# First graph: weights, splits and mask spread over four places and GpSimd; last graph: late low parts on VectorE, output projection in two parts

## The chip, the cores and the metric

The kernel runs on one core of one Trainium2 chip. A core has TensorE (PE) for matrix products, VectorE (DVE), ScalarE (ACT) and GpSimd (POOL) for elementwise work, and SyncE (SP), which here issues every DMA. The engines run their own instruction streams in order and wait for each other by semaphores. The metric is the device time of one execution in microseconds (us); lower is better.

## The reference

Two layers over 32 graphs of 512 nodes with 512 features, in float32. Cut to what matters:

```python
def layer0(x, adj, W, a):                 # W: 512 x 256
    h = x @ W                             # 512 x 256
    e = leaky_relu(h @ a[0] + (h @ a[1]).T, 0.2) + (-1e9) * (1 - adj)
    out = softmax(e) @ h
    return concatenate([out, h], -1)      # 512 x 512
def layer1(x, adj):                       # 8 heads of 64
    q, k, v = (heads(x @ Wn.T + bn) for n in "qkv")
    s = where(adj == 0, -inf, q @ k.T / 8)
    return (softmax(s) @ v).merge_heads() @ Wo.T + bo
x = layernorm(x + layer0(x, adj, W, a))
x = layernorm(x + layer1(x, adj))
```

## The kernel before, in words

Every operand of a product is split into a high part (rounded to fp32r) and a low part (the rest), and a product is three products: high by high, high by low, low by high (`PARTS`). ScalarE makes the high part (`split_hi`), VectorE or GpSimd the low part by a subtraction. Tokens lie in four tiles of 128 nodes, features in four chunks.

The work on a graph is cut into pieces with short names. The order in which each engine does them is written out by hand in tables: `TENSOR_PLAN`, `SCALAR_PLAN`, `VECTOR_PLAN`, `GPSIMD_PLAN` and `SP_PLAN` for a middle round, `LAST_..._PLAN` for the last graph, `..._PROLOGUE` and `..._START` for the first graph, `..._ENDING` for what follows the last graph. Rounds overlap: a round does attention of one graph (layer 1), the first layer of the next and the first loads of the one after.

Pieces that matter here, first layer: `A` splits the transposed input tile, `B` is `x @ W` (h, and the two attention terms from 2 extra columns of the weight), `N` spreads one term over all partitions, `pre` adds and leaks, `red` applies the mask and takes the row maximum, `aexp` is exp, `C` transposes and splits, `D` multiplies by h, `lst`/`lrs` are layer statistics, `lap` applies the layer norm, `E` transposes the result. `w0` to `w3` split Wq, Wk, Wv and Wo. Second layer: `q`, `k`, `V`, `W` are projections (`V` and `W` are the two halves of v), `scores` the products of two heads with one query tile, `reduce` mask and row maximum, `exp` the exponential, `vt` VectorE's 32 by 32 block transpose. Probabilities are finished in eight groups a graph (ph 0 to 7, four tiles each). `sv` stores a group to DRAM and `mv` loads it back turned; `hi` and `lo` split it (two instructions of 1024 columns each a group); `weigh` multiplies by v (two a group, 16 matmuls each group's pair); `lows`, `sum`, `norm` and `turn` add the halves, divide and split the result into `oT`. `O0` to `O3` are the output projection, `evO` adds it to the tokens, `yst`/`yrs` are the second layer's statistics, `fin` applies them and the tile is stored.

Waits that matter: `weigh` of group ph needs both `lo` of the group and, at its first half, the `sum` of the group before; the fourth `vt` of group ph needs the `weigh` of group ph-2 done, and `hi` needs the `weigh` of the group before done, since `turned_hi_prob` is one buffer. `load_sums` (`rl`) of group ph waits for `norm` of ph-1.

At the start, W and `a` are loaded, VectorE forms the extra weight columns with eight reductions, ScalarE splits W, VectorE makes its low part, then the mask of four tiles from `adj`. The four weights come one after another through two places: `tokens[2]` (after the mask was built from it) and `blocked[:, 0]`; each load waits for the low part of an earlier one. ScalarE has `w0 w1` at the end of `SCALAR_START`, ahead of piece `N`, and VectorE has them ahead of `red0`. A bias product `bb` (bv times Wo) stands ahead of `E0` on PE.

## Time and profile before

| | us |
|---|---|
| median of 3 runs | 3027.59 (3025.34 to 3031.99) |
| profiled execution, its own time | 3028.9 |
| span of the profiled execution | 3027.1 |
| PE busy | 2937.6 (97%) |
| DVE busy | 2611.6 (86%) |
| ACT busy | 2417.9 (80%) |
| POOL busy | 1996.2 (66%) |
| mean granted TensorE clock | 0.989 |

The busy time of PE is modelled from pipelined matmuls, so 97% says that PE hardly ever waits, not that it is at its peak. In the 40 slices of the page PE shows 9 tenths in all but the first and the last (5 and 5). The rest of the text is on these two slices, of 75.7 us each, and on what lies between them.

### The profile page before, as it was taken

What the parts mean: (1) busy time and instruction counts of PE and PEld (TensorE: products, weight loads), DVE (VectorE), ACT (ScalarE), POOL (GpSimd) and SP (SyncE); (2) the same over time, 40 slices, a digit from 0 to 9 for tenths busy, and PEclk for the clock granted to TensorE, in tenths of its full rate; (3) what the DMA queues carried; (4) which work ended last, traced back from release to release, by engine and by line L of the source; (5) the groups of instructions that cost most, each with busy time, mean ns of one, the idle gap of its engine ahead of it and who ended that gap; (6) DMA issues with size and microseconds to landing.
All of it is one profiled execution on the core that took longest, in us unless ns stands there. A gap on an engine that the chain in (4) does not pass through costs nothing.

```text
span 3027.1 us, 58284 instructions
## 1 busy us (share of the span) xinstructions
PE 2937.6 (97%) x19084; PEld 2507.9 (83%) x19084; DVE 2611.6 (86%) x6556; ACT 2417.9 (80%) x5031; POOL 1996.2 (66%) x1415
## 2 busy tenths in 40 slices
...
GB/s 132 206 224 232 239 242 231 225 225 233 237 250 228 224 226 229 243 243 230 221 222 235 239 243 227 229 225 240 238 238 223 228 235 232 242 236 227 218 210 149
DMA packets 306413, 685.39 MB, mean 226 GB/s; under 512 B 56896, under 2 KB 90432, under 8 KB 273344
## 3 DMA queue, kind: packets, MB, share of 16 engines
...
## 4 chain that ended last, share of the span: by engine, by line
PE 82%; DMA 5%; ACT 4%; DVE 4%; POOL 3%; issue 2%; SPq 1%; ACTq 0%; DVEq 0%; POOLq 0%
PE R_bank L646 47%; PE O_bank L735 14%; PE S_bank L716 11%; PE L_bank L646 6%; PE L_bank L637 3%; DMA turned_lo_prob<-scratch 3%; POOL turned_lo_prob L1093 2%; DVE blocked L1033 1%; DMA r_wide<-r_scratch 1%; DVE prob L1013 1%; ACT turned_hi_prob L764 1%; DMA scratch<-blocked 1%; ACT prob L852 1%; ACT tokens L781 1%; SPq L567 1%
## 5 line engine op out<-in xcount | busy, mean ns | idle before, releaser
L1093 POOL TENSOR_TENSOR turned_lo_prob<-turned_lo_prob,turned_hi_prob 128x1024 fp32r<-128x1024 f32 x512 | 1230.0, 2425 | 493.0 <-ACT turned_hi_prob L764 492.5
L852 ACT ACTIVATE prob<-prob,small_cols 128x512 f32<-128x512 f32 x1024 | 728.4, 715 | 89.4 <-DVE small_cols L1013 86.1
L1033 DVE STREAM_TRANSPOSE blocked<-prob 128x512 f32<-128x512 f32 x1024 | 697.6, 699 | 54.1 <-PE O_bank L735 34.7
L1013 DVE CUSTOM_DVE_ANT_0 prob<-S_bank,mask 128x512 f32<-128x512 f32 x1024 | 669.4, 681 | 31.6 <-PE S_bank L716 27.7
L735 PE MATMUL O_bank<-turned_hi_prob,v_st 128*128 128x256 f32 x2048 | 521.2, 291 | 32.7 <-POOL turned_lo_prob L1093 32.4
L764 ACT ACTIVATE turned_hi_prob<-turned_lo_prob 128x1024 fp32r<-128x1024 f32 x512 | 522.0, 1051 | 31.1 <-DMA turned_lo_prob<-scratch 27.7
L735 PE MATMUL O_bank<-turned_lo_prob,v_st 128*128 128x256 f32 x2048 | 507.8, 285 | 0.0
L735 PEld LDWEIGHTS O_bank<-turned_hi_prob,v_st 128*128 128x128 f32 x2048 | 394.1, 192 | 58.9 <-POOL turned_lo_prob L1093 52.3
L716 PE MATMUL S_bank<-qk_pair 64*128 64x512 f32 x3072 | 435.5, 411 | 6.8 <-DVE small_cols L1013 5.4
L646 PE MATMUL R_bank<-wv,x1T 128*128 128x256 f32 x3072 | 398.7, 285 | 0.0
L735 PEld LDWEIGHTS O_bank<-turned_lo_prob,v_st 128*128 128x128 f32 x2048 | 394.9, 193 | 3.9
L646 PEld LDWEIGHTS R_bank<-wv,x1T 128*128 128x128 f32 x3072 | 377.6, 189 | 12.5 <-issue 12.4
L646 PE MATMUL R_bank<-wo,oT 128*128 128x512 f32 x1536 | 382.3, 401 | 1.3 <-POOL oT L1107 1.3
L646 PE MATMUL R_bank<-x1T,wq 128*128 128x512 f32 x1536 | 379.9, 396 | 1.0 <-DVE v_st L909 1.0
L646 PE MATMUL R_bank<-x1T,wk 128*128 128x512 f32 x1536 | 380.2, 396 | 0.7 <-DVE v_st L909 0.7
L1107 POOL TENSOR_TENSOR oT<-o_half,oT 128x256 fp32r<-128x256 f32 x256 | 189.5, 740 | 244.5 <-ACT oT L764 244.1
L716 PEld LDWEIGHTS S_bank<-qk_pair 64*128 64x128 f32 x3072 | 266.8, 185 | 100.5 <-issue 27.5
L646 PEld LDWEIGHTS R_bank<-x1T,wk 128*128 128x128 f32 x1536 | 288.9, 188 | 72.3 <-DVE v_st L909 1.1
L646 PEld LDWEIGHTS R_bank<-wo,oT 128*128 128x128 f32 x1536 | 280.5, 188 | 75.5 <-issue 11.1
L646 PEld LDWEIGHTS R_bank<-x1T,wq 128*128 128x128 f32 x1536 | 282.3, 188 | 62.1 <-issue 1.4
L777 ACT ACTIVATE qk_pair<-R_bank,b_cols 128x512 fp32r<-128x512 f32 x256 | 172.4, 684 | 171.0 <-PE R_bank L646 169.6
L1087 POOL TENSOR_TENSOR o_half<-o_half,r_wide 128x256 f32<-128x256 f32 x256 | 189.1, 739 | 103.1 <-DVE o_half L1041 95.4
...
## 6 DMA issues: line engine op xcount, KB each, us to landing
scratch<-blocked SPq DMA_DIRECT2D x256, 1024.0 KB, 4.3
turned_lo_prob<-scratch SPq DMA_DIRECT2D x256, 1024.0 KB, 5.8
tokens<-xT SPq DMA_DIRECT2D x128, 256.0 KB, 5.2
tokens<-x SPq DMA_DIRECT2D x128, 256.0 KB, 2.9
r_wide<-r_scratch SPq DMA_DIRECT2D x512, 64.0 KB, 3.2
out<-tokens SPq DMA_DIRECT2D x128, 256.0 KB, 4.2
r_scratch<-r_cols SPq DMA_DIRECT2D x256, 16.0 KB
...
```

Of the source, the lines that this page charges most:

```text
L637: last = pe.transpose(bank[:, c * P:(c + 1) * P], src[:, c * P:(c + 1) * P], ident[:, :])
L646: last = pe.matmul(dst, stationary(s, c), moving(m, c), start=(c, s, m) == todo[0], stop=(c, s, m) == todo[-1])
L716: last = pe.matmul(score_bank(R, 2 * u + w)[:, :], qk_pair[own, qp, t * P:(t + 1) * P], qk_pair[own, 2 + kp, :], start=j == 0, stop=j == 2)
L735: last = pe.matmul(O_bank[:, o_cols(w)], v_st[:, c, (2 * (ph // 2) + w) % HEADS, :], probs, start=(c, s) == todo[0], stop=(c, s) == todo[-1])
L764: act.activation(dst, src, ACT.Copy).then_inc(done, 1)
L777: act.activation(hi_ap, bank_ap, ACT.Identity, bias=b_col[:, pair % 4:pair % 4 + 1]).then_inc(qk_hi, 1)
L852: act.activation(prob_tile(R, s), prob_tile(R, s), ACT.Exp, bias=negmax[:, slot:slot + 1], scale=-1.0, accum_out=psum_row[:, ph % 2, j:j + ...
L1013: dve.tensor_tensor_reduce(prob_tile(R, s), score_bank(R, s)[:, :], mask[:, s % 8 // 2, :], -SCALE, HUGE, ALU.add, ALU.min, negmax[:, slot ...
L1033: dve.transpose(blocked[:, ph % 2, :, :, 2 * (s % 2) + s % 4 // 2, :].rearrange("p d c i -> p c d i"), prob_tile(R, s).rearrange("p (d c i ...
L1087: pool.tensor_tensor(o_half[:, :], o_half[:, :], r_wide[:, :], ALU.mult).then_inc(o_normed, 1)
L1093: pool.tensor_tensor(lo_ap, lo_ap.bitcast(F32), turned_hi_prob[:, 2 * a:2 * a + 2, :, :].bitcast(F32), ALU.subtract).then_inc(p_lo, 1)
L1107: pool.tensor_tensor(oT[:, LO, u // 2 % 4, o_cols(u % 2)], o_half[:, :], oT[:, HI, u // 2 % 4, o_cols(u % 2)].bitcast(F32), ALU.subtract). ...
```

## The change

First graph. The four weights get four staging places, `blocked[:, 0]`, `blocked[:, 1]`, `tokens[1]` and `tokens[2]`, and a semaphore each. `adj`, Wv and Wq are issued right behind the first inputs, the small biases last. GpSimd builds the mask and the low parts of W (its first 256 columns), Wq and Wo; VectorE makes the low parts of the four input tiles, of Wk and of Wv. ScalarE touches its activation table at the very start, and splits the first 256 columns of W before the extra columns are known. `w0` to `w3` move behind the first layer's `pre` and `aexp`. The addition to the tokens (`X`) no longer stands between the pieces `B`. The bias product `bb` moves behind the first scores, into `O_bank`.

Last graph. For groups 4 to 7 the low part of the probabilities is made by VectorE (`vlo`) and not by GpSimd. O0 to O3 stand together ahead of `weigh0`. Ahead of the last two `weigh`, PE does three of the four chunks of the final output projection (`P0` to `P2`, then `P3`) into the score banks, which are free by then, and `O0` to `O3` are the fourth chunk alone. The last statistics are in two halves (`yrs`, `yrs1`), so that `fin0` and `fin1` need only tiles 0 and 1.

The middle rounds' tables are as they were.

```diff
@@ tables (a few of the lines)
-    "w0 w1",
+    "X0 X1 X2 X3",
-GPSIMD_START = (
-    "A0 A1 A2 A3",
-)
+GPSIMD_START = ()
 SCALAR_PROLOGUE = (
-    "N pre0 pre1 pre2 aexp0 aexp1 C0 w2",
+    "N pre0 pre1 pre2 aexp0 aexp1 C0 pre3",
+    "C1 aexp2 aexp3 C2 w2 C3 w0 w1",
...
 GPSIMD_PROLOGUE = (
-    "lrs A0 A1 bo0 A2 bo1 bo2 A3",
-    "bo3",
+    "lrs w0 w3 A0 A1 A2 A3 bo0",
+    "bo1 bo2 bo3",
 TENSOR_ENDING = (
-    "weigh weigh O0 O1 O2 O3",
+    "P0 P1 P2 weigh weigh P3 O0 O1",
+    "O2 O3",
 VECTOR_ENDING = (
-    "sum evO0 evO1 yst0 evO2 yst1 yst2 evO3",
-    "yst3 yrs0",
+    "sum evO0 evO1 yst0 yst1 evO2 evO3 yrs",
+    "yst2 yst3 yrs1",
+DVE_WEIGHTS = (1, 2)
+LAST_LO = 8
@@ staging
+        def weight_stage(j):
+            if j % 2 == 1:
+                return (blocked[:, 0, :, :, :, :].rearrange("p d c j i -> p (d c j i)").rearrange("p (c n) -> p c n", c=C),
+                        tokens[2][:, :, :])[j // 2]
+            return (tokens[1][:, :, :],
+                    blocked[:, 1, :, :, :, :].rearrange("p d c j i -> p (d c j i)").rearrange("p (c n) -> p c n", c=C))[j // 2]
@@ sync
-            for j, w in enumerate((WqT, WkT, WvT, WoT)):
-                if j == 0:
-                    sp.wait_ge(mask_built, 1 + T)
-                else:
-                    sp.wait_ge(w_lo, j)
-                place = tokens[2][:, :, :] if j % 2 == 0 else stage().rearrange("p (c n) -> p c n", c=C)
...
+            load_weight(2, WvT)
+            load_weight(0, WqT)
+            for i in range(T):
+                load_tokens(start, i)
+            sp.wait_ge(w_lo[0], 2)
+            load_weight(1, WkT)
+            sp.wait_ge(mask_built, 1 + T)
+            load_weight(3, WoT)
@@ tensor
                 if kind == "N":
                     pe.wait_ge(terms_ready, R.nx(4, 4))
-                    pe.wait_ge(solo_done, R.nx(len(SOLO), 4))
+                    if not R.prologue:
+                        pe.wait_ge(solo_done, R.nx(len(SOLO), 4))
...
+                if kind == "P":
+                    if i == 0:
+                        pe.wait_ge(s_red, R.n(32, 0))
+                        pe.wait_ge(o_lo, R.n(8, -2))
+                    for c in range(C - 1):
+                        for s, m in PARTS:
+                            pe.matmul(S_bank[i][:, :], oT[:, s, c, i * P:(i + 1) * P], wo[:, m, c, :],
+                                      start=(c, s, m) == (0,) + PARTS[0], stop=False)
+                if kind == "O" and R is end:
+                    pe.wait_ge(o_lo, R.n(8, i // 2 - 1))
+                    for s, m in PARTS:
+                        last = pe.matmul(S_bank[i][:, :], oT[:, s, C - 1, i * P:(i + 1) * P], wo[:, m, C - 1, :],
+                                         start=False, stop=(s, m) == PARTS[-1])
+                    last.then_inc(ring_mm, 1)
@@ scalar
+            act.wait_ge(mask_built, 1)
+            act.activation(a_sum[:, :], minus_half[:, :], ACT.Copy).then_inc(act_ready, 1)
             act.wait_ge(w_loaded[0], 16)
+            split_hi(w0[:, HI, :, 0:F1], w_stage()[:, :, 0:F1], w_hi[0])
             act.wait_ge(wa_done, 2 * C)
-            split_hi(w0[:, HI, :, :], w_stage(), w_hi)
-            act.wait_ge(small_loaded, SMALL)
+            split_hi(w0[:, HI, :, F1:F1 + 2], w_stage()[:, :, F1:F1 + 2], w_hi[0])
@@ vector
+                if kind == "A" and R is start:
+                    dve.wait_ge(turned_hi, R.n2(4, i + 1))
+                    split_lo(turned_part(R, "A", i, LO), tokens[R.buffer(2)][:, i, :].rearrange("p (c t) -> p c t", c=C),
+                             turned_part(R, "A", i, HI), turned_lo)
...
+            def probs_lo(R, m):
+                if m == LAST_LO:
+                    dve.wait_ge(p_lo, R.n(16, m))
+                ph, a = m // 2, m % 2
+                dve.wait_ge(p_hi, R.n(16, m + 1))
+                split_lo(turned_lo_prob[:, ph % 2, 2 * a:2 * a + 2, :, :],
+                         turned_lo_prob[:, ph % 2, 2 * a:2 * a + 2, :, :].bitcast(F32),
+                         turned_hi_prob[:, 2 * a:2 * a + 2, :, :], p_lo)
@@ gpsimd
+                if kind == "w" and i not in DVE_WEIGHTS:
+                    w = (wq, wk, wv, wo)[i]
+                    pool.wait_ge(w_hi[1 + i], 1)
+                    pool.tensor_tensor(w[:, LO, :, :], weight_stage(i), w[:, HI, :, :].bitcast(F32),
+                                       ALU.subtract).then_inc(w_lo[1 + i], 1)
...
-            pool.wait_ge(small_loaded, SMALL)
+            pool.wait_ge(w_hi[0], 1)
+            pool.tensor_tensor(w0[:, LO, :, 0:F1], w_stage()[:, :, 0:F1], w0[:, HI, :, 0:F1].bitcast(F32),
+                               ALU.subtract).then_inc(w_lo[0], 1)
+            pool.wait_ge(adj_loaded, 16)
             pool.wait_ge(mask_built, 1)
+            for t in range(T):
+                pool.tensor_scalar(turned_keys(mask[:, t, :]), by_key_place(tokens[2][:, t, :].bitcast(I32)), 0.0, MASKED,
+                                   ALU.is_equal, ALU.mult).then_inc(mask_built, 1)
```

ScalarE in the first graph, from the high parts of h on. Before (`wq`, `wk`, `wv` are the weights' high parts, `n_wide` is piece N, `prob` the first layer's attention, `x1T` pieces C):

```order
L764 ACTIVATE h<-S_bank 128x256 [waits solo_mm] x4
L764 ACTIVATE wq<-tokens 128x2048 [waits w_loaded1]
L764 ACTIVATE wk<-blocked 128x2048 [waits w_loaded2]
L813 ACTIVATE n_wide<-L_bank 128x512 [waits n_mm]
L809 ACTIVATE prob<-n_wide,terms 128x512 [waits n_copied]
L809 ACTIVATE prob<-n_wide,terms 128x512 x2
L816 ACTIVATE prob,a_cols<-prob,a_cols 128x512 [waits a_red] x2
L764 ACTIVATE x1T<-L_bank 128x4x128 [waits solo_mm]
L764 ACTIVATE wv<-tokens 128x2048 [waits w_loaded3]
```

Now:

```order
L796 ACTIVATE h<-S_bank 128x256 [waits solo_mm] x4
L847 ACTIVATE n_wide<-L_bank 128x512 [waits n_mm]
L843 ACTIVATE prob<-n_wide,terms 128x512 [waits n_copied]
L843 ACTIVATE prob<-n_wide,terms 128x512 x2
L850 ACTIVATE prob,a_cols<-prob,a_cols 128x512 [waits a_red] x2
L796 ACTIVATE x1T<-L_bank 128x4x128 [waits solo_mm]
L843 ACTIVATE prob<-n_wide,terms 128x512 [waits solo_mm]
L796 ACTIVATE x1T<-L_bank 128x4x128 [waits solo_mm]
L850 ACTIVATE prob,a_cols<-prob,a_cols 128x512 [waits a_red] x2
L796 ACTIVATE x1T<-L_bank 128x4x128 [waits solo_mm]
L796 ACTIVATE wv<-blocked 128x2048 [waits w_loaded3]
L796 ACTIVATE x1T<-L_bank 128x4x128 [waits solo_mm]
```

The high parts of Wq and Wk stood between h and `n_wide`; now no weight stands ahead of the second `x1T`, and Wv, Wq, Wk and Wo come in one stretch after the attention of the first layer.

TensorE at the end of the program. Before (`turned_lo_prob` with `v_st` is the last `weigh`, `wo` with `oT` the output projection):

```order
L735 MATMUL O_bank<-turned_lo_prob,v_st 128x256
L646 MATMUL R_bank<-wo,oT 128x512 [waits o_lo,ring_done]
L646 MATMUL R_bank<-wo,oT 128x512 x8
L646 MATMUL R_bank<-wo,oT 128x512 [waits o_lo]
L646 MATMUL R_bank<-wo,oT 128x512 x2
L646 MATMUL R_bank<-wo,oT 128x512 [waits ring_done]
L646 MATMUL R_bank<-wo,oT 128x512 x11
L646 MATMUL R_bank<-wo,oT 128x512 [waits ring_done]
L646 MATMUL R_bank<-wo,oT 128x512 x11
L646 MATMUL R_bank<-wo,oT 128x512 [waits ring_done]
L646 MATMUL R_bank<-wo,oT 128x512 x11
```

Now, from the last matmul of `weigh13` to the first of `weigh14`, and from `P3` on:

```order
L767 MATMUL O_bank<-turned_lo_prob,v_st 128x256
L722 MATMUL S_bank<-wo,oT 128x512 [waits o_lo,s_red]
L722 MATMUL S_bank<-wo,oT 128x512 x26
L767 MATMUL O_bank<-turned_hi_prob,v_st 128x256 [waits o_sum,p_lo]
...
L767 MATMUL O_bank<-turned_lo_prob,v_st 128x256
L722 MATMUL S_bank<-wo,oT 128x512 x9
L727 MATMUL S_bank<-wo,oT 128x512 [waits o_lo]
L727 MATMUL S_bank<-wo,oT 128x512 x2
L727 MATMUL S_bank<-wo,oT 128x512 [waits o_lo]
L727 MATMUL S_bank<-wo,oT 128x512 x2
L727 MATMUL S_bank<-wo,oT 128x512 [waits o_lo]
L727 MATMUL S_bank<-wo,oT 128x512 x2
```

Of 48 matmuls of the last output projection 36 moved ahead of the last `oT` half: 27 stand between `weigh13` and `weigh14`, 9 behind `weigh15`; 12 are left behind the wait for `o_lo`.

VectorE at the same place. Before (`r_cols` is the inverse of the row sums, `o_half` the `sum` pieces):

```order
L1041 TENSOR_TENSOR o_half<-O_bank,o_half 64x4x2x32 [waits o_lows] x2
L1022 RECIPROCAL r_cols<-psum_row 128x4 [waits p_exp,r_stored]
L1024 STREAM_TRANSPOSE r_cols<-r_cols 128x32 [waits p_inv]
L1033 STREAM_TRANSPOSE blocked<-prob 128x4x4x32 [waits p_exp] x2
L1033 STREAM_TRANSPOSE blocked<-prob 128x4x4x32 [waits p_exp,pv_mm]
L1022 RECIPROCAL r_cols<-psum_row 128x4 [waits p_exp,r_stored]
L1024 STREAM_TRANSPOSE r_cols<-r_cols 128x32 [waits p_inv]
L1041 TENSOR_TENSOR o_half<-O_bank,o_half 64x4x2x32 [waits o_lows] x6
```

Now:

```order
L1082 STREAM_TRANSPOSE blocked<-prob 128x4x4x32 [waits p_exp,pv_mm]
L1071 RECIPROCAL r_cols<-psum_row 128x4 [waits p_exp,r_stored]
L1073 STREAM_TRANSPOSE r_cols<-r_cols 128x32 [waits p_inv]
L945 TENSOR_TENSOR turned_lo_prob<-turned_lo_prob,turned_hi_prob 128x1024 [waits p_hi] x2
L1090 TENSOR_TENSOR o_half<-O_bank,o_half 64x4x2x32 [waits o_lows] x4
L1071 RECIPROCAL r_cols<-psum_row 128x4 [waits p_exp,r_stored]
L1073 STREAM_TRANSPOSE r_cols<-r_cols 128x32 [waits p_inv]
L945 TENSOR_TENSOR turned_lo_prob<-turned_lo_prob,turned_hi_prob 128x1024 [waits p_hi] x2
L1090 TENSOR_TENSOR o_half<-O_bank,o_half 64x4x2x32 [waits o_lows] x2
```

Two low parts (`turned_lo_prob`) stand ahead of `sum5` and `sum6`, and two more ahead of `sum7`.

## Rows read from the trace of the kernel before

**Rows 1.** The page: busy time of each engine, share, instructions.

```profile
PE 2937.6 (97%) x19084; PEld 2507.9 (83%) x19084; DVE 2611.6 (86%) x6556; ACT 2417.9 (80%) x5031; POOL 1996.2 (66%) x1415
```

**Rows 2.** Busy time, clock (PEclk) and DMA in three stretches of 20 us.

```profile
120.00:140.00 20.00, 20.00 (x142) 17.72 (x142) 18.26 (x45) 16.14 (x36) 12.09 (x10) 1.00 0.58 199
2840.00:2860.00 20.00, 20.00 (x133) 17.67 (x132) 17.35 (x44) 14.80 (x29) 11.62 (x8) 1.00 0.54 198
2980.00:3000.00 20.00, 5.96 (x28) 5.46 (x27) 2.77 (x7) 6.24 (x10) 10.46 (x8) 0.59 0.52 188
```

**Rows 3.** Timeline, 0 to 60: start, duration, instruction, idle before and its releaser.

```profile
10.41 1.28 ACT L764 ACT_TABLE_LOAD   x1 [10.41 <-DVE blocked L1067]
...
12.68 2.17 ACT L764 ACTIVATE x1T<-tokens 128x512 fp32r<-128x512 f32 x4
...
15.31 7.60 PE L646 MATMUL S_bank<-w,x1T 128*128 128x258 f32 x48 [15.31 <-POOL x1T L1113]
...
26.31 1.91 ACT L764 ACTIVATE wq<-tokens 128x2048 fp32r<-128x2048 f32 x1 [2.98 <-DMA tokens<-WqT]
...
30.78 0.58 ACT L813 ACTIVATE n_wide<-L_bank 128x512 f32<-128x512 f32 x1
...
33.12 1.02 DVE L958 CUSTOM_DVE_ANT_1 prob<-prob,mask 128x512 f32<-128x512 f32 x1
...
54.06 1.52 ACT L781 ACTIVATE tokens<-tokens,scale_cols 128x512 f32<-128x512 f32 x2 [5.89 <-POOL scale_cols L1102]
```

**Rows 4.** Timeline, 60 to 104: first scores, first store, first weigh.

```profile
73.38 1.65 PE L716 MATMUL S_bank<-qk_pair 64*128 64x512 f32 x12 [0.23 <-DVE qk_pair L930]
...
83.30 0.43 SPq L545 DMA_DIRECT2D scratch<-blocked  x1
...
100.63 0.58 PE L735 MATMUL O_bank<-turned_hi_prob,v_st 128*128 128x256 f32 x1 [0.39 <-POOL turned_lo_prob L1093]
```

**Rows 5.** Instructions of the whole run by line and form (busy, mean ns).

```profile
L1093 POOL TENSOR_TENSOR turned_lo_prob<-turned_lo_prob,turned_hi_prob 128x1024 fp32r<-128x1024 f32 x512 | 1230.0, 2425 | 493.0 <-ACT turned_hi_prob L764 492.5
...
L764 ACT ACTIVATE turned_hi_prob<-turned_lo_prob 128x1024 fp32r<-128x1024 f32 x512 | 522.0, 1051 | 31.1 <-DMA turned_lo_prob<-scratch 27.7 <-PE O_bank L735 0.8
...
L1113 POOL TENSOR_TENSOR turned<-tokens,turned 128x512 fp32r<-128x512 f32 x124 | 161.3, 1300 | 47.8 <-ACT turned L764 47.8
...
L909 DVE TENSOR_TENSOR x1T<-L_bank,x1T 128x512 fp32r<-128x512 f32 x132 | 91.3, 691 | 39.8 <-ACT x1T L764 36.5
...
L1073 DVE TENSOR_SCALAR mask<-tokens 128x512 bf16<-128x512 int32 x4 | 6.6, 1719 | 0.0
L1113 POOL TENSOR_TENSOR x1T<-tokens,x1T 128x512 fp32r<-128x512 f32 x4 | 6.6, 1678 | 11.9 <-ACT x1T L764 11.9
...
L1067 DVE CUSTOM_DVE_ANT_0 n_wide<-blocked,alpha 128x256 f32<-128x256 f32 x8 | 3.4, 424 | 6.0 <-DMA alpha<-a 5.8
...
L909 DVE TENSOR_TENSOR wq<-tokens,wq 128x2048 fp32r<-128x2048 f32 x1 | 2.3, 2293 | 4.1 <-ACT wq L764 4.1
```

**Rows 6.** Timeline of PE, the last waits for low parts and the projection.

```profile
2968.06 0.58 PE L735 MATMUL O_bank<-turned_hi_prob,v_st 128*128 128x256 f32 x1 [3.37 <-POOL turned_lo_prob L1093]
...
2990.35 0.58 PE L735 MATMUL O_bank<-turned_hi_prob,v_st 128*128 128x256 f32 x1 [8.17 <-POOL turned_lo_prob L1093]
...
3001.54 0.58 PE L735 MATMUL O_bank<-turned_hi_prob,v_st 128*128 128x256 f32 x1 [7.41 <-POOL turned_lo_prob L1093]
...
3008.89 9.37 PE L646 MATMUL R_bank<-wo,oT 128*128 128x512 f32 x39 [1.28 <-POOL oT L1107]
```

**Rows 7.** Chain of waits, the last store and load on it.

```profile
2973.62 3.84 DMA scratch<-blocked
...
2977.47 6.96 DMA turned_lo_prob<-scratch
```

**Rows 8.** Timeline, after the last projection: ScalarE and VectorE.

```profile
3018.36 0.69 DVE L1001 TENSOR_TENSOR tokens<-R_bank,tokens 128x512 f32<-128x512 f32 x1 [0.50 <-PE R_bank L646]
...
3021.67 2.93 ACT L781 ACTIVATE tokens<-tokens,scale_cols 128x512 f32<-128x512 f32 x4 [13.64 <-POOL scale_cols L1102]
```

157 lines of the change are left out of this document (87 added, 70 removed), and 48 rows, old and new, of tables (LAST_GPSIMD_PLAN, LAST_SP_PLAN, LAST_VECTOR_PLAN, SCALAR_PROLOGUE).

## The prediction

> **What bounds the kernel now.** I read the busy times of the page first: PE 2937.6 of 3027.1 us [rows 1]. Two middle stretches of 20 us then tell how firmly PE holds it: 20.00 busy of 20.00 at 120 and again at 2840, at full clock [rows 2]. So between them nothing is to be had, and nothing changes there; but time gained before 120 is handed on whole, since PE then only starts its unbroken work earlier, and time gained after about 2900 ends the program earlier. PE is idle 3027.1 - 2937.6 = 89.5 us, nearly all at the two ends. From 2980 to 3000 it is busy 5.96 of 20.00 at a mean clock of 0.59 [rows 2].
>
> The timeline of the start comes next. The first matmul starts at 15.31, released by a low part on GpSimd. PE has then its four B pieces done by 22.91, yet ScalarE copies their result (`n_wide`) only at 30.78: it had been sent to wait for Wq (26.31, after 2.98 idle) and then split two weights. The first masked row maximum is at 33.12 and the first layer norm at 54.06 [rows 3]. First scores: 73.38; first probability store: 83.30; first `weigh`: 100.63 [rows 4].
>
> Last, the timeline of PE in the last graph: it waits 3.37, 8.17 and 7.41 us for low parts made by GpSimd, at `weigh` 8, 12 and 14, and after 1.28 more runs 39 matmuls of the projection in 9.37 [rows 6]; then statistics, GpSimd and four ScalarE tiles follow in a row up to 3021.67 + 2.93 = 3024.60 [rows 8].
>
> **Start, step by step.** (a) First matmul. The eight reductions end where the table load begins, 10.41. After it stood the table load 1.28 and W's high part, up to 12.68 [rows 3]. Now the load and 256 of 258 columns are done earlier; left are a split of 8 columns (estimate 0.2, from none up to a fifth of the 1.0 us it was part of), an input tile's high part (2.17 / 4, and 0.61 for the first alone) and its low part on VectorE, 0.69 [rows 5], with three waits of about 0.05: 10.41 + 0.2 + 0.6 + 0.7 + 0.1 = 12.0, so 3.3 earlier. GpSimd's low part of W runs beside the reductions (2.4 [rows 5], from about 6) and is hidden.
>
> Here VectorE and GpSimd meet. In the trace GpSimd's 128x512 subtraction takes 1678 ns beside the mask on VectorE and 1300 ns otherwise [rows 5], 29% more. The Trainium skill (GPSIMD Engine Reference, "Key points") says that the two share their SBUF interfaces and collide when VectorE has two SBUF inputs or runs in a 2-port mode; by that rule the eight reductions, which have two such inputs, would themselves slow down beside GpSimd. If they took the same 29% on 8 x 0.424 [rows 5], 1.0 us would come back. The trace agrees as to GpSimd and shows no pair for the other direction, so the sum leaves it out and the range holds it.
>
> (b) The B pieces stay PE's own, 7.6 us, to 19.6. High and low part of h and the terms 0.9, `N` and its copy 1.3, one `pre` 0.7: `red0` at 22.5, where it was at 33.12: 10.6 gained. It also needs the mask, now on GpSimd, and `X0` to `X3` (4 x 0.43 behind the terms, till 22.2; their loads are issued by 14). `adj` stands four issues earlier in the queue, and I take it as landed at 11. GpSimd's price for a mask tile is in no row: from below 1.3, its two-input time at this size; from above 4, well over double VectorE's 1.72 [rows 5]. I take 1.7. Then tile 0 is there at 13 and tile 3 at 18; at 4 they come at 15 and 27, just when `red3` wants it. So nothing, with 3 us to lose at the upper end.
>
> (c) `red0` to layer norm was 54.06 - 33.12 = 20.9, in which VectorE made two weights' low parts (2 x 2.29 [rows 5]) and PE waited between `C` and `D`. Now VectorE has none. Chain: three `red` 3.0, `C0` copy and split with `pre3` 1.5, `red3` 1.1, C1, D0 cold 3.5, C2, D1, C3, D2, D3 about 6.8, last statistics 1.8, GpSimd 1.3: 19.0 at most, so 41.5. ScalarE has its four weights (4 x 1.91) in the same stretch, from 32, and with two splits comes to 40.6. I take 40.6: 13.4 gained. So the weights' high parts are what bounds now, and a faster chain would bring under 1 us.
>
> (d) Layer norm to first scores was 19.3. `B0` leaves it (1.5), VectorE's low part of Wv and Wk come in (hidden behind the E pieces: 41.3 against 42.5, and 52.7 before `k4` at 53.3). GpSimd's Wq and Wo take 4.7 each (2 x 2.4), to 49; `q4` wants Wq at 50.5. First scores 59.4: 14.0 gained. (e) Behind them ScalarE has `B1 A2` ahead of the first `exp`, and PE has the bias product, 12 matmuls of 0.24, in the stretch up to `k1`. The store goes at 69.6, 13.7 gained, `k1` ends 12 earlier. The first `weigh` needs both: **12 gained at the start**. Bounds: 8 (mask at 4 us, contention, cold clock for all of C and D) to 14.5.
>
> **End, step by step.** PE has the same work up to `scores12`, only in another order: `weigh0` and `weigh1` go 4 us later, behind O2 and O3, and `weigh4`, whose chain hangs on `weigh1`, then has its low parts about when PE comes to it. No gain, no loss; up to 3 us of loss if that chain is late. (f) Groups 4 to 7: a pair of low parts costs 2 x 2.4 on GpSimd; on VectorE half of 2.29 and a little, 1.2 each [rows 5]: 2.4 less per pair. But VectorE has queued work ahead of it. `vlo8` stands behind three `reduce` of scores that come at 2961, so `weigh8` starts at 2967.0 instead of 2968.06. `weigh9` now follows at once, without scores between: its end goes from 2972.8 to 2970.4. Group 6 hangs on that: fourth `vt` 0.8, store 3.84, load 6.96 [rows 7], high part 1.05 [rows 5], low parts; the store-to-load part is unchanged, the pair 2.4 shorter, but `sum5` now stands behind `vlo13` and `weigh12` needs it, 0.9 back. 2.4 + 2.4 - 0.9 = 3.9: `weigh12` at 2986.5. (g) `weigh13` then ends at 2990.2 (3.7 at the low clock). Before, 7.41 of idle time followed. Now PE does 27 matmuls of the projection at 9.37 / 39 = 0.24: 6.5, while VectorE's `sum6`, `vlo14`, `vlo15` take 5.4, so PE itself becomes the bound. `weigh14` at 2996.7, 4.9 earlier, and as PE comes to it busy it runs at 2.4 GHz, not 1.2 as after the wait: 2.0 and not 3.8. Its end 6.6 earlier; the load of the sums for `norm7` may take back some. (h) From the last `oT`: before, 39 matmuls, and 3024.60 - 3008.89 = 15.7 to the last tile. Now 3 matmuls and a start (1.1), two `evO` 1.3, two `yst` 1.6, two `evO` 1.3, `yrs` 0.3, two `yst` 1.6, `yrs1` 0.3, GpSimd 1.3, two ScalarE tiles 1.5: 10.3. VectorE is the bound there. 5.4 gained. **End: 6.6 + 5.4 = 12.** Bounds: 7 (no gain in f, half in g, all of h less 1) to 16.
>
> **Sum.** 12 + 12 = 24. The profiled execution took 3028.9 (span 3027.1 and 1.8 around it), 1.3 over the median; from the median, 3027.6 - 24 = 3003.6. With both ends at their bounds 15 to 30.5; I reach a little further below for a loss that I have not seen.
>
> The Trainium skill (ScalarE: Activation LUTs, "What ACT_TABLE_LOAD costs") gives 1283 ns for the load and some 1380 ns of drain behind it. The trace has the load at 1.28, but the next ACTIVATE within 0.02 of its end, so the row decides and the estimate of 1.4 more by that page is not in the sum; with it the time would be 3002.2.
>
> **Rivals.** First, VectorE clogs in the last graph: eight low parts are 9.7 us of new work on an engine that works in order, and each `vlo` stands ahead of a `vt`, `reduce` or `sum` while it waits for ScalarE. For it: `vlo8` ahead of `vt24`, `sum5` behind `vlo13`. Against: from 2980 to 3000 VectorE is busy 2.77 of 20 [rows 2]. Then (f) and (g) give nothing and only (h) stays: 3027.6 - 12 - 5.4 = 3010.2. Second, GpSimd or ScalarE is late at the start (Wq's low part late for `q4`, four high parts late for the layer norm), and only (a) and the idle part of (b) are kept, 6: 3027.6 - 6 - 12 = 3009.6. For it: ScalarE's 7.6 us of splits in one stretch. Third, the gain at the start doesn't carry, as the middle is not really held by PE: 3015.6. Against it the two full stretches. Fourth, slower: a mask tile on GpSimd, reading every fourth int32, is many times dearer than my bound. It costs from 4 us a tile on, and eats all 24 from (27 + 24 - 11) / 4 = 10 us a tile: 3028 and more; at 12 us 3036. Nothing near it is in the rows; an unseen form is all that speaks for it. That the change doesn't do what it says can't well be: order and waits stand in the program.
>
> **Chances.** The forecast 0.72, VectorE clogged 0.11, late at the start 0.10, not carried 0.03, slower 0.02, and 0.02 for more gained than 30. About 0.2% (6 us) is what a measurement of this kernel can tell. Faster by more than that: all but the last two small parts, 0.96; within 0.2%: 0.02; slower 0.02. Range 2996 to 3014: it holds the forecast with nearly all of its bounds and the first two rivals.
>
> **What would show it.** (a) the first matmul near 12.0; (b) `red0` near 22.5 and released by ScalarE, not by the mask; (c) the first layer norm at 40.6, straight behind a weight's high part; (d) first scores near 59.4; (e) the first `weigh` near 88.6; PE still 20.00 of 20 in the middle; (f, g) no PE wait of over 3 us between the projection's 27 matmuls and `weigh14`; (h) 10.3 from the last `oT` to the last tile. Wrong would be: a wait for the mask in front of `red`, a wait of `q4` for GpSimd, PE idle before `scores12`, or idle time of PE in the middle that before had none.

## The result, and the profile after

The kernel after takes 3011.74 us (median of 5 runs, 3011.38 to 3012.9), before 3027.01 in the same set; the ratio is 0.995, 95% interval 0.9938 to 0.9961. So the change gained 15.3 us where 24 were forecast. The profiled execution took 3012.9, with a span of 3011.1, 16.0 shorter than before.

The middle is as full as in [rows 2], and the last stretch is filled, as the windows of the kernel after show (busy time of PE, PEld, DVE, ACT and POOL, clock, DMA):

```profile
120.00:140.00 20.00, 20.00 (x138) 16.85 (x137) 18.17 (x47) 17.38 (x35) 12.75 (x9) 1.00 0.62 212
2840.00:2860.00 20.00, 20.00 (x146) 18.27 (x145) 17.35 (x44) 15.16 (x31) 11.39 (x9) 1.00 0.58 192
2980.00:3000.00 20.00, 15.88 (x74) 13.81 (x74) 7.76 (x13) 7.26 (x12) 4.02 (x6) 0.83 0.49 172
```

The timeline of its start, with the instructions of [rows 3, 4]:

```profile
5.75 2.34 POOL L1208 TENSOR_TENSOR w<-blocked,w 128x1024 fp32r<-128x1024 f32 x1 [4.21 <-ACT w L796]
6.33 2.05 DVE L1127 CUSTOM_DVE_ANT_0 n_wide<-blocked,alpha 128x256 f32<-128x256 f32 x1 [5.47 <-DMA alpha<-a]
...
11.82 10.00 POOL L1213 TENSOR_SCALAR mask<-tokens 128x512 bf16<-128x512 int32 x4 [3.73 <-DMA tokens<-adj]
11.93 1.02 DVE L945 TENSOR_TENSOR w<-blocked,w 128x8 fp32r<-128x8 f32 x1 [0.28 <-ACT w L796]
...
13.69 8.74 PE L662 MATMUL S_bank<-w,x1T 128*128 128x258 f32 x48 [13.69 <-DVE x1T L945]
...
25.50 1.05 DVE L1003 CUSTOM_DVE_ANT_1 prob<-prob,mask 128x512 f32<-128x512 f32 x1 [0.80 <-ACT prob L843]
...
41.42 2.29 DVE L945 TENSOR_TENSOR wv<-blocked,wv 128x2048 fp32r<-128x2048 f32 x1
41.60 3.00 POOL L1154 TENSOR_TENSOR scale_cols<-scale_cols,small_cols 128x4 f32<-128x4 f32 x1 [19.78 <-DVE scale_cols L957]
44.91 1.52 ACT L815 ACTIVATE tokens<-tokens,scale_cols 128x512 f32<-128x512 f32 x2 [2.45 <-POOL scale_cols L1157]
45.78 1.12 PE L653 MATMUL L_bank<-ident,tokens 128*128 128x128 f32 x4 [6.18 <-ACT tokens L815]
...
49.15 2.91 PE L662 MATMUL R_bank<-wv,x1T 128*128 128x256 f32 x12
...
66.25 0.96 PE L746 MATMUL S_bank<-qk_pair 64*128 64x512 f32 x6
...
96.03 0.58 PE L767 MATMUL O_bank<-turned_hi_prob,v_st 128*128 128x256 f32 x1 [0.40 <-POOL turned_lo_prob L1148]
```

The first `weigh` is at 96.03, 4.6 earlier than in [rows 4], not 12. Three things strike: a reduction of 2.05 us where the other seven still take 0.42; GpSimd's power on 128x4 (the first of the two small instructions behind the layer statistics) at 3.00 us where the kernel before has 1.02; and V0 at 2.91 us, which is the low clock: the granted clock reads 0.50 in every stretch of 2 us from 44 to 56. In the kernel before, TensorE had the bias product in this wait, idled 1.95 and did `E0` at the high clock:

```profile
50.00 2.97 PE L646 MATMUL S_bank<-wo,oT 128*128 128x512 f32 x12
...
54.93 0.66 PE L637 MATMUL L_bank<-ident,tokens 128*128 128x128 f32 x4 [1.95 <-ACT tokens L781]
```

The timeline of PE and ScalarE at the end, against [rows 6, 8]:

```profile
2963.28 0.58 PE L767 MATMUL O_bank<-turned_hi_prob,v_st 128*128 128x256 f32 x1 [4.90 <-DVE turned_lo_prob L945]
2975.06 0.58 PE L767 MATMUL O_bank<-turned_hi_prob,v_st 128*128 128x256 f32 x1 [5.50 <-DVE turned_lo_prob L945]
2984.12 0.55 PE L767 MATMUL O_bank<-turned_hi_prob,v_st 128*128 128x256 f32 x1 [5.28 <-DVE o_half L1090]
2987.68 7.28 PE L722 MATMUL S_bank<-wo,oT 128*128 128x512 f32 x27
...
2996.70 2.25 PE L722 MATMUL S_bank<-wo,oT 128*128 128x512 f32 x9
2998.79 3.32 PE L727 MATMUL S_bank<-wo,oT 128*128 128x512 f32 x12
...
3007.07 1.52 ACT L815 ACTIVATE tokens<-tokens,scale_cols 128x512 f32<-128x512 f32 x2 [0.36 <-POOL scale_cols L1157]
```

Here PE goes from the 27 matmuls straight into `weigh14` (2994.80), with no wait, and behind the last `oT` there are 12 matmuls at most where there were 39.

**A ruler for both ends.** ScalarE copies the neighbour terms (`n_wide`) once per graph, 32 times. These rows cut a span into a start (to the copy for the second graph), a middle and an end (from the last copy). In the kernel before, then after:

```profile
91.13 0.58 ACT L813 ACTIVATE n_wide<-L_bank 128x512 f32<-128x512 f32 x1
...
2826.40 0.60 ACT L813 ACTIVATE n_wide<-L_bank 128x512 f32<-128x512 f32 x1
```

```profile
86.52 0.58 ACT L847 ACTIVATE n_wide<-L_bank 128x512 f32<-128x512 f32 x1
...
2822.57 0.60 ACT L847 ACTIVATE n_wide<-L_bank 128x512 f32<-128x512 f32 x1
```

Start 91.1 and 86.5, end 3027.1 - 2826.4 = 200.7 and 188.5: 4.6 gained at the start, 12.2 at the end, and 0.8 lost in the middle. The middle, the same code in all, took 2733.9 to 2742.5 us over the profiled executions of this text (the first of its 30 graphs 88.0 to 89.0, the others 90.9 to 93.0), so single times say little below some 4 us, while start and end say more. They scatter too: where the code of the start is the same it took 85.7 to 86.8 (five executions, new start) and 91.1 and 92.5 (old start), and the new end took 187.1 to 190.3. One profile stands behind each line, so a difference of under some 1.5 at the start or 3 at the end decides nothing by itself.

"Median" is the median time of a kernel's executions. The profiled execution can be some us off it (start_only 3025.8 for 3020.2). The kernels were timed in five sets, the last four on four chips: before and after; start_only, end_only, pow_first and w_after_reds; no_overlap, filler, lows_gpsimd and proj_late; combo, combo_warm and after_again; combo_warm2. The kernel before took 3027.01, 3026.36, 3026.15, 3026.14 and 3026.46 in them, but the kernel after 3011.74 in the first and 3007.39 in the fourth, so medians are compared within a set.

| kernel | start | middle | end | median |
|---|---|---|---|---|
| before | 91.1 | 2735.3 | 200.7 | 3027.01 |
| after | 86.5 | 2736.1 | 188.5 | 3011.74 |
| after_again | 86.0 | 2736.6 | 188.5 | 3007.39 |
| start_only | 86.3 | 2738.8 | 198.9 | 3020.22 |
| end_only | 92.5 | 2734.4 | 188.7 | 3014.02 |
| pow_first | 89.7 | 2734.4 | 188.3 | 3011.86 |
| w_after_reds | 84.9 | 2742.5 | 188.8 | 3010.84 |
| no_overlap | 82.6 | 2737.2 | 190.3 | 3007.66 |
| filler | 85.5 | 2733.9 | 187.7 | 3007.40 |
| lows_gpsimd | 85.7 | 2736.9 | 196.8 | 3018.84 |
| proj_late | 86.8 | 2736.8 | 195.7 | 3014.74 |
| combo | 81.5 | 2736.2 | 188.2 | 3007.73 |
| combo_warm | 84.6 | 2736.6 | 187.1 | 3010.05 |
| combo_warm2 | 79.0 | 2734.5 | 188.7 | 3004.21 |

### The profile page after: what moved, and what is told of

Its sections match the earlier page's. It is cut to its first block, busy times and chain, and to the rows that moved or that the text cites. A ratio compares the mean times of both kernels' runs of the same rounds, so it can differ in the third digit from the quotient of the medians.

```text
span 3011.1 us, 58295 instructions
## 1 busy us (share of the span) xinstructions
PE 2936.8 (98%) x19084; PEld 2509.5 (83%) x19084; DVE 2616.8 (87%) x6564; ACT 2423.5 (80%) x5033; POOL 1997.8 (66%) x1412
## 3 DMA queue, kind: packets, MB, share of 16 engines
q1 hardware_dynamic: 306112, 681.68, 65.5%
## 4 chain that ended last, share of the span: by engine, by line
PE 84%; DMA 4%; ACT 3%; DVE 3%; POOL 2%; issue 1%; SPq 1%; ACTq 0%; DVEq 0%; POOLq 0%
PE R_bank L662 47%; PE O_bank L767 15%; PE S_bank L746 12%; PE L_bank L662 6%; PE L_bank L653 4%; DMA turned_lo_prob<-scratch 3%; POOL turned_lo_prob L1148 2%; DVE blocked L1082 1%; DMA r_wide<-r_scratch 1%; ACT turned_hi_prob L796 1%; DVE prob L1062 1%; ACT prob L886 1%; SPq L583 1%; DMA scratch<-blocked 1%; ACT tokens L815 0%
## 5 line engine op out<-in xcount | busy, mean ns | idle before, releaser
L1148 POOL TENSOR_TENSOR turned_lo_prob<-turned_lo_prob,turned_hi_prob 128x1024 fp32r<-128x1024 f32 x504 | 1211.6, 2426 | 477.2 <-ACT turned_hi_prob L796 476.8
L662 PEld LDWEIGHTS R_bank<-wv,x1T 128*128 128x128 f32 x3072 | 378.9, 189 | 12.6 <-issue 11.7
L662 PE MATMUL R_bank<-wo,oT 128*128 128x512 f32 x1488 | 370.2, 401 | 0.0
L662 PEld LDWEIGHTS R_bank<-wo,oT 128*128 128x128 f32 x1488 | 270.9, 188 | 72.2 <-issue 11.1
```

The lines of the kernel that those rows point to most:

```text
L662: last = pe.matmul(dst, stationary(s, c), moving(m, c), start=(c, s, m) == todo[0], stop=(c, s, m) == todo[-1])
L1148: pool.tensor_tensor(lo_ap, lo_ap.bitcast(F32), turned_hi_prob[:, 2 * a:2 * a + 2, :, :].bitcast(F32), ALU.subtract).then_inc(p_lo, 1)
```

## The experiments

**The two halves apart.** start_only takes the last graph's tables, the endings and their branches back; end_only is the kernel before with those alone.

> The kernel after with the last graph, the endings and their helpers put back as before; only the first graph is new. Theory (the first graph gained 4.6 us at the first weigh, of which 3.6 are left at k1 of the last graph, and the last graph the other 12.4): 3027.0 - 3.6 = 3023.4 us; first layer norm 44.9, first weigh 96.0 as in the kernel after; the tail with its waits of 3.4, 8.2 and 7.4 us back. Rival (the first graph is worth the 12 us of the forecast, and the order of the last graph gave some of it back): 3015 us.

> The kernel before with only the last graph, the endings and their helpers new. Theory: the gain of the last graph stands by itself, 3027.0 - 12.4 = 3014.6 us, with the first weigh at 100.6. Rival (part of the last graph's gain needs the earlier arrival of the work from the start, as in weigh0 at full clock): 3018 us or more, with a longer wait at weigh8 or weigh10 than the kernel after had.

Measured: 3020.22 (ratio 0.9977, 0.9968 to 0.9986) and 3014.02 (0.9957, 0.9944 to 0.9969). The halves are independent within the scatter: start 86.3 with the old end, end 188.7 with the old start. The rival that the start is worth 12 falls, as the interval allows 4.2 to 9.7. It also misses the 3.6 us of the theory by a little; the start by the ruler is 4.8.

**Who stretched what.** pow_first:

```diff
                     if i in DVE_WEIGHTS:
                         dve.wait_ge(w_hi[1 + i], 1)
+                        if i == 2:
+                            dve.wait_ge(ln_pool[0], 2)
```

> The kernel after, with VectorE's low part of Wv waiting until GpSimd's two small instructions of the first layer norm are done. Theory (VectorE's 2.29 us subtraction stretched GpSimd's pow on 128x4 from 1.0 to 3.0 us): pow 1.0 us, first layer norm at 42.9 instead of 44.9, Wv's low part done at 45.2 and not waited for, first scores and first weigh 2.0 earlier, 3009.8 us. Rival (pow is slow by itself after 19.8 us without work on GpSimd): pow stays at 3.0, first layer norm at 44.9, Wv's low part at 47.2, 3011.7 us or a little more.

w_after_reds, on GpSimd:

```diff
             pool.wait_ge(w_hi[0], 1)
+            pool.wait_ge(wa_done, 2 * C)
             pool.tensor_tensor(w0[:, LO, :, 0:F1], ...)
```

> The kernel after, with GpSimd's low part of W waiting until VectorE's eight reductions are done. Theory (GpSimd's subtraction stretched VectorE's first reduction from 0.42 to 2.05 us): all eight at 0.42, the last ends at 10.05 instead of 11.6; W's low part then runs from 10.1 to 12.5, so the first matmul is at about 12.6 instead of 13.69 and the time 3010.7 us. Rival (the first reduction is slow by itself, as the first custom instruction): it stays at 2.05, W's low part ends at 14.0, first matmul at 14.1, 3012.1 us.

In pow_first the power takes 1.04 us, as expected, and the layer norm comes at 42.87. But the start got 3.2 us longer, and the time is 3011.86: the number of the rival, whose cause (a power that is slow by itself) the 1.04 rules out. Its timeline of VectorE, then of GpSimd:

```profile
42.94 6.54 DVE L945 TENSOR_TENSOR wv<-blocked,wv 128x2048 fp32r<-128x2048 f32 x1 [1.50 <-POOL scale_cols L1159]
```

```profile
41.52 1.04 POOL L1156 TENSOR_TENSOR scale_cols<-scale_cols,small_cols 128x4 f32<-128x4 f32 x1 [19.72 <-DVE scale_cols L957]
...
42.78 4.54 POOL L1171 TENSOR_TENSOR wq<-tokens,wq 128x2048 fp32r<-128x2048 f32 x1
47.25 6.69 POOL L1171 TENSOR_TENSOR wo<-tokens,wo 128x2048 fp32r<-128x2048 f32 x1
```

GpSimd started 0.16 before VectorE and ran at its own pace, to 47.32; VectorE, with 2.29 us of work, ended at 49.48, and 47.32 + 2.29 = 49.61. Then it was GpSimd's turn to be late by 2.1. So for these instructions it is no sharing of bandwidth: one stands still until the other's instruction is over. In w_after_reds all eight reductions take 0.42, and the instruction behind them pays:

```profile
10.13 2.26 DVE L945 TENSOR_TENSOR w<-blocked,w 128x8 fp32r<-128x8 f32 x1 [0.28 <-ACT w L796]
```

In combo, further down, the same eight columns take 0.17; here GpSimd had W from 10.00 to 12.35, and 12.35 + 0.17 is within 0.15 of the end, 12.39. The first matmul came at 13.13, not 12.6. The start gained 1.6 of its 86.5, which is barely more than scatter: 0.4 was left of it at the layer norm, the rest came in E and V pieces that ran at the high clock (V1 1.67 for 2.68), though no edit touches them. The time, 3010.84, agrees with the 3010.7 of the theory, but a median can't tell 1 us from none.

The same sum holds in the kernel after: Wv's low part ends at 43.71, and the power, 1.0 of work, at 44.60. VectorE's splits from PSUM, with one SBUF input, stayed at 0.69 beside Wq on GpSimd. The Trainium skill (SBUF — State Buffer, "Who interferes with whom") states this: the shared pair is an exclusive lock, whoever issues first holds it for the whole instruction, and a VectorE instruction with two SBUF inputs contends with a GpSimd instruction that reads SBUF. On these pairs the traces agree to 0.15 us; on the mask, and once on which of two waiting instructions goes first, they do not, as told below and in the last section.

**Both waits placed, and the clock.** no_overlap is pow_first and, on GpSimd, a wait of Wq's low part for Wv's:

```diff
                     pool.wait_ge(w_hi[1 + i], 1)
+                    if i == 0:
+                        pool.wait_ge(w_lo[3], 1)
```

> The kernel after, with VectorE's low part of Wv waiting for GpSimd's two small instructions of the first layer norm, and GpSimd's low part of Wq waiting for VectorE's low part of Wv, so that no two of these overlap. Theory (a VectorE instruction with two SBUF inputs and a GpSimd instruction exclude each other for their whole length; that is what made Wv's low part 6.54 us in pow_first): pow 1.0, Wv's low part 2.3 from 42.9, Wq's 4.5 from 45.2 and Wo's 4.6, first layer norm at 42.9, first scores at 64.2 and first weigh at 94.0 (2.0 earlier than after), 3009.7 us. Rival (the chain behind the layer norm has other limits, as Wq's low part for q4 or a colder TensorE): first scores at 66 or later, 3011.7 us.

filler gives TensorE work that nobody reads:

```diff
-    "D3 E0 E1 V0 E2 E3 V1 q4",
+    "D3 F E0 E1 V0 E2 E3 V1 q4",
+                if kind == "F":
+                    for _ in range(40):
+                        pe.matmul(O_bank[:, 0:F1], x1T[:, HI, 0, 3 * P:4 * P], h0[:, HI, 0, :], start=True, stop=True)
```

> The kernel after, with 40 matmuls more (128x128 by 256 columns into O_bank, read by nobody) between D3 and E0, in the 6.18 us where TensorE waits for the first layer norm. Theory (the cold clock made the E and V pieces longer): the extra matmuls take 5.6 us at 2.4 GHz and end before the layer norm; then E transposes at 0.63 instead of 1.1, V0 and V1 at 1.68 instead of 2.9 and 2.7, first scores near 62.3 instead of 66.25, first weigh near 92.1, 3007.8 us. Rival (this stage is held by ScalarE and VectorE, and the clock is worth little, or the extra matmuls run cold, 9.6 us, and are in the way): first scores at 65.5 or later, 3011 us or more.

no_overlap: first scores at 62.29, first `weigh` at 92.09, the start 3.9 shorter. That is more than the 2.0 expected. Of it 2.0 are the power, 0.7 were gained ahead of the power, and 1.2 came behind `E0`, since the last pieces (V1 1.68) ran at 2.4 GHz. The last 1.2 can't be credited to the edit, as w_after_reds has them too. The reductions and W's low part, as they fell in this execution, show both orders in one place (VectorE, then GpSimd):

```profile
5.77 0.42 DVE L1129 CUSTOM_DVE_ANT_0 n_wide<-blocked,alpha 128x256 f32<-128x256 f32 x1 [4.92 <-DMA alpha<-a]
...
6.24 2.44 DVE L1129 CUSTOM_DVE_ANT_0 n_wide<-blocked,alpha 128x256 f32<-128x256 f32 x1
```

```profile
5.78 2.62 POOL L1212 TENSOR_TENSOR w<-blocked,w 128x1024 fp32r<-128x1024 f32 x1 [4.25 <-ACT w L796]
```

The first reduction was there 0.01 before GpSimd, kept its 0.42 and made GpSimd 0.3 late (2.62 for 2.34); the second then stood until GpSimd was done.

filler: first scores at 65.21, where the theory had 62.3 and the rival 65.5 or later, so the theory of this run fails, and the timeline of PE shows why:

```profile
45.07 0.66 PE L653 MATMUL L_bank<-ident,tokens 128*128 128x128 f32 x4 [1.49 <-ACT tokens L818]
47.23 1.08 PE L653 MATMUL L_bank<-ident,tokens 128*128 128x128 f32 x4 [1.51 <-DVE x1T L948]
47.97 2.91 PE L662 MATMUL R_bank<-wv,x1T 128*128 128x256 f32 x12
```

E0 was fast, and it came after a wait of 1.49 us; the granted clock is 1.00 up to 46, 0.58 from 46 to 48 and 0.50 from 48 on. So not the first wait of 1.5 us cost the clock but the next, before `E1`. The start gained 1.0 against one profile of the kernel after and 0.5 against the other; that decides nothing. The median, 3007.40, is nearly the 3007.8 of the theory, but by luck: no_overlap in the same set took 3007.66 with a start 2.9 shorter, and the kernel after itself took 3007.39 in the next set.

**All of it.** combo is no_overlap with W's low part on VectorE, ahead of the reductions; combo_warm adds 30, 10 and 10 such matmuls before E0, E1 and E3; after_again is the kernel after, once more beside them.

```diff
             dve.wait_ge(w_loaded[0], 16)
+            dve.wait_ge(w_hi[0], 1)
+            split_lo(w0[:, LO, :, 0:F1], w_stage()[:, :, 0:F1], w0[:, HI, :, 0:F1], w_lo[0])
-    "D3 E0 E1 V0 E2 E3 V1 q4",
+    "D3 F30 E0 F10 E1 V0 E2 F10 E3 V1 q4",
```

> no_overlap, and the low part of W's 256 columns on VectorE ahead of its eight reductions instead of on GpSimd beside them. Theory (exclusion): the subtraction takes 1.15 us from 5.7, the reductions end at 10.6, the low part of the 8 columns is 0.1 to 0.2 us and not 1.02, the first matmul starts at 12.0 instead of 13.69, first weigh at 90.5 (92.1 in no_overlap), 3006.2 us. Rival (the 1.15 us in front of the reductions cost all that the exclusion cost): first matmul at 13 or later, 3007.7 us.

> combo, and matmuls that nobody reads in TensorE's waits of the first layer norm and behind it: 30 before E0, 10 before E1, 10 before E3. Theory (the filler run failed because 1.5 us of waiting stayed before E0 and again before E1, and TensorE was at 1.2 GHz again): E1 and E2 at 0.63, V0 at 1.68 instead of 2.91, first scores 2 us earlier than in combo, first weigh at 88.5, 3004.2 us. Rival (ScalarE and VectorE hold this stage, and fillers delay the pieces behind them): first scores as in combo or later, 3006.2 us or more.

> The kernel after unchanged, beside the two above on the same chip. All theories: 3011.7 us, first weigh at 95.5 to 96.1, 188.5 us from ScalarE's copy of the neighbour terms for the last graph to the end; the middle between differs by up to some us from one execution to the next.

combo: first matmul at 12.27, the 8 columns 0.17, first scores 61.18, first `weigh` 90.97 (90.5 expected), start 81.5. So the rows are those of the theory, while its time, 3007.73, is the number of the rival. The times of combo and after_again, 3007.73 and 3007.39, don't tell the two apart; after itself differs by 4.4 between its two sets. combo_warm kept the clock (V0 1.68) and lost 3.1 at its start all the same, against its theory (3010.05 for 3004.2). Its VectorE, PE and GpSimd:

```profile
50.67 5.82 DVE L950 TENSOR_TENSOR wk<-blocked,wk 128x2048 fp32r<-128x2048 f32 x1
```

```profile
56.97 4.57 PE L664 MATMUL R_bank<-x1T,wk 128*128 128x512 f32 x12 [3.09 <-DVE v_st L950]
```

```profile
48.46 4.65 POOL L1180 TENSOR_TENSOR wo<-tokens,wo 128x2048 fp32r<-128x2048 f32 x1
53.07 1.27 POOL L1184 TENSOR_TENSOR turned<-tokens,turned 128x512 fp32r<-128x512 f32 x1
```

GpSimd had Wo from 48.46 to 53.11 and an input tile to 54.34; 54.34 + 2.29 = 56.63, and Wk ended at 56.49. Here VectorE, waiting since 50.67, was passed by an instruction that GpSimd started at 53.07; in pow_first it got in between two of GpSimd's. So "who comes first" does not tell who goes next, and what does is not shown. Faster pieces had brought VectorE into GpSimd's stretch. combo_warm2 takes that away:

```diff
-                    if i == 0:
-                        pool.wait_ge(w_lo[3], 1)
+                    pool.wait_ge(w_lo[3 if i == 0 else 2], 1)
-    "lrs w0 w3 A0 A1 A2 A3 bo0",
+    "lrs w0 A0 w3 A1 A2 A3 bo0",
```

> combo_warm, with GpSimd's low part of Wo behind VectorE's low part of Wk and behind its own first input tile. In combo_warm the fillers did keep the clock (V0 1.68, k4 could have started at 53.9), but Wk's low part met Wo's on GpSimd, 48.46 to 53.11, and the input tile's, to 54.34, and took 5.82 us. Theory (exclusion, taken away here): Wk's low part 2.3 us, to 53.0; k4 at 53.9 without a wait, first scores at 59.7 (61.2 in combo, 64.3 in combo_warm, 66.0 in the kernel after), first weigh at 89.4, about 6.5 us earlier than in the kernel after; with its 188 at the end and a middle of 2736, some 3004 us. Rival (something else holds k4, or Wo's low part is now late for the bias product and delays k1): first scores at 62 or later, or a wait at the bias product, 3007 us.

```profile
43.74 0.63 PE L655 MATMUL L_bank<-ident,tokens 128*128 128x128 f32 x4 [0.41 <-DVE x1T L950]
44.12 1.68 PE L664 MATMUL R_bank<-wv,x1T 128*128 128x256 f32 x12
...
58.76 0.96 PE L751 MATMUL S_bank<-qk_pair 64*128 64x512 f32 x6
...
88.52 0.58 PE L772 MATMUL O_bank<-turned_hi_prob,v_st 128*128 128x256 f32 x1 [0.39 <-POOL turned_lo_prob L1157]
```

Wk's low part is 2.28, k4 follows q4 at 52.99, and the granted clock of 40 to 60 is 1.00, 0.66 in the kernel after (combo_warm2, then after):

```profile
40.00:60.00 20.00, 18.57 (x124) 16.02 (x123) 10.49 (x14) 9.34 (x17) 12.79 (x6) 1.00 0.22 66
40.00:60.00 20.00, 11.21 (x50) 10.02 (x51) 9.33 (x13) 9.61 (x14) 12.87 (x5) 0.66 0.15 53
```

The first `weigh` is at 88.52, 7.5 earlier than after; 3004.21 us (3001.57 to 3006.07), ratio to before 0.9925 (0.9912 to 0.9939). It is the lowest median here, but its interval overlaps those of after (0.9938 to 0.9961) and after_again (0.993 to 0.9955); what is clear of scatter is the start, 79.0 for 86.5 and 86.0. From its E0 to the first scores it takes 17.3 us, the kernel after 20.5.

**The last graph.** lows_gpsimd drops the eight `vlo` from VectorE's table and puts four pairs `lo lo` into GpSimd's; proj_late changes one line:

```diff
-    "P0 P1 P2 weigh weigh P3 O0 O1",
+    "weigh weigh P0 P1 P2 P3 O0 O1",
```

> The kernel after, with the low parts of weigh groups 4 to 7 of the last graph back on GpSimd (two of 2.4 us each for a pair instead of 2.36 together on VectorE); projection in two parts and the two-part layer norm kept. Theory (they are worth part of the last graph's gain): weigh8 2.4 us later, weigh14 about 3 later and again after a long wait, so at the low clock, end 4 us later, 3015.7 us. By the forecast's steps f and g it would be 6.6, 3018.3 us. Rival (VectorE's part of the low parts hides nothing, the chains of stores and loads hold the groups): 3011.7 us.

> The kernel after, with P0, P1 and P2 (27 matmuls of the output projection) behind the last two weighs instead of ahead of them. Theory (they fill a wait, and keep the clock up for weigh14 and weigh15): weigh14 starts 2 us earlier but at the low clock and ends at the same time, then 36 and 3 matmuls instead of 9 and 3 stand ahead of the first evO: 6.3 us later, 3018.0 us. Rival (the wait ahead of weigh14 is not really free, as weigh14 is released 2 us before TensorE is done with P): end only 4 us later or less.

By the ruler lows_gpsimd loses 8.3 at the end and proj_late 7.2. Their medians, 3018.84 and 3014.74, are 11.4 and 7.3 above filler, which in the same set has the new end and nearly their start. Both losses are above what was expected (4 or 6.6, and 6.3). In lows_gpsimd `weigh8`, `10`, `12` and `14` are 3.0, 4.8, 6.2 and 8.2 later than after (both have the last copy at 2822.57). The first and last of its waits on PE, for low parts on GpSimd:

```profile
2966.27 0.58 PE L768 MATMUL O_bank<-turned_hi_prob,v_st 128*128 128x256 f32 x1 [7.21 <-POOL turned_lo_prob L1149]
...
3003.02 0.39 PE L768 MATMUL O_bank<-turned_hi_prob,v_st 128*128 128x256 f32 x1 [1.98 <-POOL turned_lo_prob L1149]
```

Each group hangs on the one before, and each adds 1.5 to 3.0 of the 2.3 us that a pair costs more on GpSimd. So the chains of stores and loads don't hide the low parts, and the rival falls. In proj_late `weigh14` came 2.0 earlier, but after a wait of 4.92 and at the low clock, and ended when it did in the kernel after; 36 matmuls then stood ahead of the first `evO`, as expected.

The two together are worth more (15.5) than the 12.2 of the end. Part of that can be read: lows_gpsimd has the low parts where the kernel before has them, and counted from the last copy its `weigh8` is at 143.7 (141.7 before) and its `weigh14` at 180.5 (175.1 before). So with low parts on GpSimd the rest of the new order loses up to 5.3 there; which piece of it does was not tried.

## Why the prediction held in its range, with the start off

The measured 3011.7 lies inside the range, and the gain is 15.3 where 24 were forecast. The start gave 4.6 for 12, below even its lower bound of 8; the end gave 12.2 for 12, but by luck, as two of its terms are off by 2.0 each way and cancel. The range held because it reached down to the sum of both lower bounds, 15.

- **(a) First matmul, 12.0 forecast, 13.69 measured.** The failed term is the contention. The prediction priced it as a share, 29% of 3.4 us, 1.0, and left it out of the sum. The 29% came from a mask instruction with one SBUF input; the reductions have two. The runs show an exclusion: 1.63 us for one reduction, so that the last ended at 11.64 and not 10.41. The 8 columns beside the mask took 0.8 more than alone, of which 0.4 came through: in lows_gpsimd, where the mask began only at 13.03, they took 0.17 and the first matmul was at 13.31. With W's low part on VectorE itself (combo) it was 12.27, which is the forecast within 0.3.
- **(b) `red0`, 22.5 against 25.50.** 1.7 come from (a); the B pieces took 8.74 and not 7.6. In executions with the same code here they took 7.9 to 8.7: what differs is how long the matmuls ran at half their later pace (about 7 a us for 11). Why is not shown; the granted clock reads 1.00 throughout. A mask tile cost 2.44 us on GpSimd (one 2.81), inside the bounds and nearer their middle than the 1.7 taken. As forecast, it was ready by 21.8 and waited for by nobody; the dear-mask rival is out.
- **(c) Layer norm, 40.6 against 44.91.** `red0` was 3.0 late, but not all of that came through: in pow_first it was 0.9 earlier than here and the power started only 0.1 earlier. ScalarE's weights ended at 42.47 and were not last: GpSimd's power was, 2.0 us late behind VectorE's low part of Wv. Each alone was cheap; that the two meet was not looked at.
- **(d) First scores, 59.4 against 66.25.** 2.5 more in the stage where 18.8 was forecast and 21.3 measured: E and V at 1.2 GHz (combo_warm2, at 2.4 GHz, takes 18.1 for the same stage). The step took the stage's length of before, in which the bias product stood in TensorE's wait (at 50.00, shown above) and `B0` behind; the change took both out and TensorE then idled 6.18. That the two kept the clock is not tested by a run of its own, and even before, `E1` ran at 1.2 GHz (1.09). Wq's and Wk's low parts were in time, as said.
- **(e)** 29.8 from first scores to first `weigh`, 29.2 forecast.
- The middle carried the gain: 4.6 at its start, 3.8 at its end, within its own scatter. The rival that it would not falls.
- **(f), (g) Low parts, 6.6 forecast.** Counted from the last copy, `weigh8` gained 0.9 (1.1 forecast), `weigh10` nothing, `weigh12` 2.4 (3.9), `weigh14` 2.9 (4.9) and the last `oT` 4.6 (6.6). So 2.0 were missing, 1.5 of them by `weigh12`. The place is `weigh10`: from the last copy, ScalarE's high parts for it started at 148.4 where they had started at 146.4, behind two exponentials that had waited 1.63 for row maxima. VectorE's pair then took 2.89 instead of 2.36, as GpSimd's `norm` came between (1.00 instead of 0.72). That is a small piece of the clogging rival. With all low parts taken back at once the end loses 8.3.
- **(h) Projection in two parts, 5.4 forecast, 7.6 measured** (8.2 from the last `oT` to the last tile, not 10.3). The step put everything behind the last `oT`. But `O0` and `O1` need only the `oT` before it: `evO0` starts at 2999.76, the last `oT` is done at 3000.39.

By the number the clogging rival came nearest, 3010.2 for 3011.7, and that is chance: it has the start at 12 and the end at 5.4. The late-at-the-start rival, 3009.6, has the split about right, 6 and 12 for 4.6 and 12.2. Its mechanism was not the one that worked: Wq's low part was late for nobody and ScalarE's high parts were not what the layer norm waited for. What made things late was low parts on one of VectorE and GpSimd in the way of the other, and the clock.

Budget of the 7.4 us by which the first `weigh` missed 88.6, as differences between the kernel after and combo_warm2: 1.4 at the first matmul, 0.9 from there to the power (not traced to a piece), 2.0 at the power, 3.2 in E and V (20.5 against 17.3). combo_warm2 gives all four back and lands on 88.52. It does so with a low part moved, three waits placed and 50 matmuls added, none of which the forecast had, so it shows what the terms cost and not that the forecast's sum was sound.
